# Perceiver-style block on one core: heads stage without its tile loop, two-half probabilities times values, GpSimd and VectorE splitting the rotary sums by Q and K, late code loads on ScalarE's queue

## What is computed

```python
x = x + xattn(layernorm(x), ctx, wq, wk, wv, wo)      # one head, 256 context rows and the 64 own rows
# 16 heads of 128, rotary, causal, 64 tokens a sequence
Q, K, V = xn @ W_Q[n] + b_Q, xn @ W_K[n] + b_K, xn @ W_V[n] + b_V
r1, r2 = x1 * cos - x2 * sin, x1 * sin + x2 * cos     # for Q and for K
probs = softmax(where(causal, Q @ K.T / sqrt(128), -inf))
x = x + (probs @ V) @ W_O + b_O
# gate, up and down weights are 4-bit codes with a scale for each group of 128
y = (silu(xn @ w_gate.T) * (xn @ w_up.T)) @ w_down.T
x = x + y / sqrt(mean(y * y) + eps)
```

## Time and profile before

| | us |
|---|---|
| median of 3 runs (1444.58 to 1448.53) | 1446.46 |
| profiled execution | 1445.04 |
| its span in the trace | 1443.2 |
| TensorE busy in the span | 1360.7 (94%) |
| VectorE busy | 980.1 (68%) |
| ScalarE busy | 508.1 (35%) |
| GpSimd busy | 425.7 (29%) |

### The profile page before, as it was taken

One profiled execution on the slowest core, in us unless ns is written; L12 is line 12 of the kernel. 1 busy time (PEld: TensorE's weight loads), 2 busy tenths in 40 slices (PEclk: granted clock), 3 DMA queues, 4 the chain that ended last, 5 costly groups with the idle time before them and its releaser, 6 DMA issues. The chain is left out here.

```text
span 1443.2 us, 24076 instructions
## 1 busy us (share of the span) xinstructions
PE 1360.7 (94%) x8964; PEld 795.3 (55%) x8964; DVE 980.1 (68%) x2176; ACT 508.1 (35%) x1249; POOL 425.7 (29%) x302
## 2 busy tenths in 40 slices
PE   8999999968999899998999999999998499999997
PEld 6666666435666566665667666654443234343433
DVE  6443443447887688776877777738829796969693
ACT  3222222322333333332343333320001483838281
POOL 0000000003333133331333333320302391929292
PEclk9999999989999999999999999999999699999999
DMA  8555555331001100101010000268550000000000
GB/s 323 218 212 211 212 196 193 118 126 54 31 28 47 61 30 31 59 16 60 31 59 30 18 28 31 89 199 244 166 157 1 0 2 29 0 29 0 29 1 30
DMA packets 59459, 122.53 MB, mean 85 GB/s; under 512 B 4312, under 2 KB 37720, under 8 KB 52696
## 3 DMA queue, kind: packets, MB, share of 16 engines
q1 hardware_dynamic: 59352, 121.07, 24.5%
HBM read 95.89 MB, written 25.17 MB: 84 GB/s over the span
## 5 line engine op out<-in xcount | busy, mean ns | idle before, releaser
L931 POOL TENSOR_TENSOR hd_rotated<-hd_products 64x512 f32<-64x512 f32 x64 | 109.3, 1708 | 725.1 <-DVE hd_products L1116 725.1
L184 PE MATMUL psum<-hd_xt_hi,hqk_hi 128*128 128x512 f16 x512 | 195.8, 382 | 1.7 <-DVE hd_xt_lo L1090 1.7
L185 PE MATMUL psum<-hd_xt_lo,hqk_hi 128*128 128x512 f16 x512 | 195.6, 382 | 0.0
L186 PE MATMUL psum<-hd_xt_hi,hqk_lo 128*128 128x512 f16 x512 | 195.2, 381 | 0.0
L1442 POOL TENSOR_TENSOR ff_part<-ff_part 128x512 f32<-128x512 f32 x88 | 127.7, 1465 | 98.0 <-DVE ff_part L1569 97.6
L184 PE MATMUL psum<-hd_wv_hi,hd_xt_hi 128*128 128x256 f16 x512 | 140.3, 274 | 4.6 <-DVE hd_wv_lo L1095 4.6
L1471 PE MATMUL psum<-ff_xt_hi,gu 128*128 128x512 f16 x352 | 133.9, 380 | 8.2 <-DVE w_rows L1607 3.3
L185 PE MATMUL psum<-hd_wv_lo,hd_xt_hi 128*128 128x256 f16 x512 | 140.3, 274 | 0.0
L186 PE MATMUL psum<-hd_wv_hi,hd_xt_lo 128*128 128x256 f16 x512 | 140.2, 274 | 0.0
L1472 PE MATMUL psum<-ff_xt_lo,gu 128*128 128x512 f16 x352 | 133.4, 379 | 0.0
L1569 DVE SCALAR_TENSOR_TENSOR ff_part<-psum,gu_scale,ff_part 128x512 f32<-128x512 f32 x176 | 119.8, 738 | 6.2 <-ACT ff_part L1519 3.6
(11 more groups left out here) (170 smaller groups left out, 2795.0 us busy)
## 6 DMA issues: line engine op xcount, KB each, us to landing
xa_kv_t<-in_ctx_t_dram SPq DMA_DIRECT2D x16, 1024.0 KB, 5.3
xa_kv<-in_ctx_dram SPq DMA_DIRECT2D x16, 1024.0 KB, 4.8
w_rows<-in_head_weights_dram SPq DMA_DIRECT2D x12, 1024.0 KB, 7.5
z_scratch<-hd_z_hi SPq DMA_DIRECT2D x32, 256.0 KB, 2.2
z_scratch<-hd_z_lo SPq DMA_DIRECT2D x32, 256.0 KB, 2.5
w_rows<-z_scratch SPq DMA_DIRECT2D x8, 1024.0 KB, 8.0
hqk_lo<-z_scratch SPq DMA_DIRECT2D x8, 1024.0 KB, 7.7
xn<-in_x_dram SPq DMA_DIRECT2D x8, 512.0 KB, 3.8
```

The source lines that it names most:

```text
L184: pe.matmul(out, lh, rh, start=(first and i == 0), stop=False)
L185: pe.matmul(out, lh, rl, start=False, stop=False)
L186: last = pe.matmul(out, ll, rh, start=False, stop=(final and i == k - 1))
L931: pool.tensor_tensor(rotated[0:HALF, w, 0, :], products[0:HALF, w, 0, :], products[0:HALF, w, 2, :], ALU.subtract)
```

## The change

The change has four parts.

- **Heads without the loop.** `for_each_step` calls the steps of all four tiles one by one. Tokens and counts are constants, and the `nop`s that followed waits on registers are gone.
- **Probabilities times values in halves.** ScalarE writes the transposed probabilities and the values as float16 (`pt_hi`, `v_hi`) and no longer frees their banks. VectorE makes the rest: `low_values` (two instructions, behind `low_top`) and `low_probs` (two instructions, between k0's and k1's products), and these free banks 5, 6 and 7. z is 24 float16 matmuls of 128 columns in place of 8 products in float32.
- **Sums.** `rotate` becomes `multiply` and `sum_up`: GpSimd makes all four sums of Q, VectorE all four of K, after k1's products. TensorE's scores wait for one count of each.
- **Late codes.** Groups 2 and 3 are loaded by two DMAs at the head of ScalarE's list, each behind `gu_decoded` alone.

The diff, cut to its core:

```diff
-        v = sb("v", [P, TT, 2 * DH], F32)
+        v_hi, v_lo = sb("v_hi", [P, TT, 2 * DH], F16), sb("v_lo", [P, TT, 2 * DH], F16)
 
         probs = sb("probs", [P, SEQS, S], F32)
 
-        probs_t = sb("probs_t", [P, 2, TT, P], F32)
...
                 for pair in range(PAIRS):
                     ends = pair == PAIRS - 1
                     step(Step(t, pair, turn_next=ends and not last_tile, proj=not (ends and last_tile), last_tile=last_tile))
-            with eng.Fori(0, NT - 1) as t:
-                tile(t, False)
-            tile(NT - 1, True)
+            for t in range(NT):
+                tile(t, t == NT - 1)
+
+        def sum_up(eng, w):
+
+            low, high = slice(0, HALF), slice(HALF, P)
+            eng.tensor_tensor(rotated[low, w, 0, :], products[low, w, 0, :], products[low, w, 2, :], ALU.subtract)
+            eng.tensor_tensor(rotated[high, w, 0, :], products[low, w, 1, :], products[low, w, 3, :], ALU.add)
+            eng.tensor_tensor(rotated[low, w, 1, :], products[high, w, 0, :], products[high, w, 2, :], ALU.subtract)
+            return eng.tensor_tensor(rotated[high, w, 1, :], products[high, w, 1, :], products[high, w, 3, :], ALU.add)
 
         block = ctx.enter_context(nc.Block())
 
...
         def _(pool):
             def step(s):
                 if not s.proj:
                     return
-                for w in range(2):
-                    banks.wait_moved(pool, s.runs_proj, ("qk"[w], 1))
-                    if not isinstance(s.t, int):
-                        pool.nop(nofuse=True)
-                    pool.tensor_tensor(rotated[0:HALF, w, 0, :], products[0:HALF, w, 0, :], products[0:HALF, w, 2, :], ALU.subtract)
-                    pool.tensor_tensor(rotated[HALF:P, w, 1, :], products[HALF:P, w, 1, :], products[HALF:P, w, 3, :],
-                                       ALU.add).then_inc(pool_rotated, 1)
-
-            for_each_step(nc.gpsimd, step)
+                banks.wait_moved(pool, s.runs_proj, ("q", 1))
+                sum_up(pool, 0).then_inc(pool_rotated, 1)
+
+            for_each_step(step)
 
         @block.tensor
         def _(pe):
...
-                    pe.wait_ge(rotated_done, s.a * 2 + 2)
-                    pe.wait_ge(pool_rotated, s.a * 2 + 2)
+                    pe.wait_ge(rotated_done, s.a + 1)
+                    pe.wait_ge(pool_rotated, s.a + 1)
                     if not s.proj:
...
                         for i in range(TT):
-                            last = pe.matmul(psum_of(unit)[:, i * P:(i + 1) * P], v[:, i, h * DH:(h + 1) * DH], probs_t[:, h, i, :],
-                                             start=True, stop=True)
+                            d = slice(h * DH, (h + 1) * DH)
+                            last = three_passes(pe, psum_of(unit)[:, i * P:(i + 1) * P], [(v_hi[:, i, d], v_lo[:, i, d])],
+                                                [(pt_hi[:, h, i, :], pt_lo[:, h, i, :])])
                         banks.fills(last, unit)
...
                     for n in range(2):
                         keys = slice(n * S, (n + 1) * S)
                         turned = psum_of(s.probs)[keys, :].rearrange("p (i h q) -> p h i q", h=2, q=S)
-                        last = act.activation(probs_t[keys, :, :, keys], turned, ACT.Copy)
-                    banks.moves(last, s.probs)
+                        last = act.activation(pt_hi[keys, :, :, keys], turned, ACT.Copy)
+                    last.then_inc(pt_hi_done, 1)
                     for h in range(2):
                         banks.wait_filled(act, s.runs_z, (s.z, h))
                         if h == 0:
                             act.wait_ge(small_loaded_z_stored, s.a * 32 + 16 * HEADS_SMALL)
-                            act.nop(nofuse=True)
                         act.activation(z_hi[:, h, :], psum_of((s.z, h)), ACT.Identity,
                                        bias=bias_v[:, s.pair * 2 + h:s.pair * 2 + h + 1]).then_inc(z_hi_done, 1)
                 if s.proj:
                     for half in range(2):
                         unit = ("v", half)
                         banks.wait_filled(act, s.runs_proj, unit)
-                        banks.moves(act.activation(v[:, 2 * half:2 * half + 2, :].rearrange("p i d -> p (i d)"), psum_of(unit), ACT.Copy,
-                                                   scale=AS / (XS * WS)), unit)
+                        act.activation(v_hi[:, 2 * half:2 * half + 2, :].rearrange("p i d -> p (i d)"), psum_of(unit), ACT.Copy,
+                                       scale=AS / (XS * WS)).then_inc(v_hi_done, 1)
                 if s.pair == WO_STEP - 1:
                     act.wait_ge(loaded[0], s.t * 16 + 32)
-                    act.activation(wo_hi[:, bass.ds(s.t * 4, 4), :].rearrange("p n m -> p (n m)"), w_rows[:, 0, :], ACT.Copy,
+                    act.activation(wo_hi[:, s.t * 4:s.t * 4 + 4, :].rearrange("p n m -> p (n m)"), w_rows[:, 0, :], ACT.Copy,
                                    scale=WS).then_inc(wo_hi_done, 1)
 
             act.wait_ge(bias_scaled, 2)
             act.wait_ge(zeros_set, 1)
 
-            for_each_step(nc.scalar, step)
+            for_each_step(step)
 
         @block.vector
         def _(dve):
...
-            def rotate(s, w):
+            def multiply(s, w):
                 for half, (first, second) in enumerate((((cos, 0), (sin, 1)), ((sin, 2), (cos, 3)))):
                     unit = ("qk"[w], half)
+                    if s.att and w == 1 and half == 1:
+                        low_probs(s)
                     banks.wait_filled(dve, s.runs_proj, unit)
                     for tab, slot in (first, second):
                         last = dve.scalar_tensor_tensor(by_sequence(products[:, w, slot, :]), by_sequence(psum_of(unit)),
                                                         bias[:, w, half, s.next_pair:s.next_pair + 1], table(tab), ALU.add, ALU.mult)
                     banks.moves(last, unit)
-                banks.wait_moved(dve, s.runs_proj, ("qk"[w], 1))
-
-                low, high = slice(0, HALF), slice(HALF, P)
-                dve.tensor_tensor(rotated[high, w, 0, :], products[low, w, 1, :], products[low, w, 3, :], ALU.add)
-                dve.tensor_tensor(rotated[low, w, 1, :], products[high, w, 0, :], products[high, w, 2, :],
-                                  ALU.subtract).then_inc(rotated_done, 1)
+
+            def low_values(s):
+                for half in range(2):
+                    unit = ("v", half)
+                    runs = {"turn": s.turns, "proj": s.a}
+                    dve.wait_ge(v_hi_done, 2 * s.a + half + 1)
+                    at = slice(2 * half, 2 * half + 2)
+                    banks.moves(dve.scalar_tensor_tensor(v_lo[:, at, :].rearrange("p i d -> p (i d)"), psum_of(unit), AS / (XS * WS),
+                                                         v_hi[:, at, :].rearrange("p i d -> p (i d)"), ALU.mult, ALU.subtract), unit)
+
+            def low_probs(s):
+                dve.wait_ge(pt_hi_done, s.a + 1)
+                for n in range(2):
+                    keys = slice(n * S, (n + 1) * S)
+                    turned = psum_of(s.probs)[keys, :].rearrange("p (i h q) -> p h i q", h=2, q=S)
+                    last = dve.tensor_tensor(pt_lo[keys, :, :, keys], turned, pt_hi[keys, :, :, keys], ALU.subtract)
+                banks.moves(last, s.probs)
 
             def while_exponentials_run(s):
                 if s.pair in (1, 2, 3) and not s.last_tile:
...
                     banks.moves(last, s.scores)
                     banks.wait_moved(dve, s.runs_scores, s.scores)
                     dve.tensor_scalar(low_top[:, :], top[:, :], -HEAD_SCALE, None, ALU.mult).then_inc(low_top_ready, 1)
+                    low_values(s)
                     while_exponentials_run(s)
                     dve.wait_ge(exp_done, s.a + 1)
                     dve.reciprocal(inv_total[:, :], total[:, :]).then_inc(inv_done, 1)
...
-                    rotate(s, 0)
-                    rotate(s, 1)
+                    multiply(s, 0)
+                    multiply(s, 1)
+                    banks.wait_moved(dve, s.runs_proj, ("k", 1))
+                    sum_up(dve, 1).then_inc(rotated_done, 1)
+                else:
+                    low_probs(s)
                 if s.att:
...
-            def load_codes(g):
-                sp.dma_start(codes[g % 2], codes_of(gu_codes, g)).then_inc(gu_loaded[g % 2], 16)
-
             def load_x1(t):
                 sp.dma_start(x2[:, t * TT:(t + 1) * TT, :],
                              x1_rows[t * TILE:(t + 1) * TILE, :].rearrange("(b p) d -> p b d", p=P)).then_inc(x1_loaded, 16)
 
             load_z(1, 0)
...
-                    if half == 0:
-                        sp.wait_ge(gu_decoded, t - 1)
-                        load_codes(t)
 
         @block.gpsimd
         def _(pool):
...
+            for g in range(2, KD):
+                act.wait_ge(gu_decoded, g - 1)
```

(3 more changed lines are left out.)

28 lines of the change are left out of this document (12 added, 16 removed).

## The result

The changed kernel takes **1434.77 us** (median of 4 runs, 1433.5 to 1435.27) against 1445.83 for the kernel before beside it (1444.58 to 1448.53): ratio 0.9919, 95% interval 0.9905 to 0.9933. It is faster, by 11 us; I had forecast 34, and the result lies 0.8 us above my range. The profiled execution took 1435.27 us; its span is 1433.5 against 1443.2, so 9.7 less. I cut both spans at three starts on TensorE.

The account below looks back on a forecast made before the run. TensorE, busy for 94% of the span, and its waits bound the kernel. Terms -13.0 - 13.7 + 18.6 + 0 - 2.0 - 23.1 - 1.0 = -34.2 took 1445.0 to 1410.8, median 1412 us; range 1393 to 1434.

Parts of the forecast that it names:

- The loop: Heads: straight code removes the surplus at the loop's two jumps, -13.0 us, bounds 0 and -13.0.
- Rival 3: Heads: straight code pauses too, since its instructions are still fetched; +13, 1425 us, chance 0.07.
- z in three passes: Heads: z's 24 matmuls of 128 columns take 1.35 us instead of 1.78, over 32 steps -13.7 us.
- rival 2: Heads: weight loads set z's pace; up to +33, 1445 us, halfway 1428; chance 0.15.
- Low halves: Heads: z waits for VectorE's `low_probs`, 0.22 us in plain steps, more in late ones; +18.6 us, bounds 0 and +37.
- Rivals 1: Heads: the low halves cost nothing, as VectorE is idle for several us of a step; 1393 us, chance 0.12.
- 5: Heads: GpSimd's sums of Q block `low_probs`; +56, 1468 us, slower than before; chance 0.05.
- Sums: Heads: sums of Q and K finish before the scores are due; 0, with 0.7 us of cover.
- First scores: Start of heads: TensorE waited 5.72 us for GpSimd's K sums; the new split ends sooner, -2.0 us.
- Feed-forward: Feed-forward's first dozen transposes run at 2.4 GHz instead of starting at the 1.2 GHz level; -1.0 us.
- Late codes: Merge: earlier code loads end VectorE's pauses and most of TensorE's 24.20 us wait; -23.1 us, bounds 0 and -24.2.
- rival 4: Merge: codes early in vain, z's loads late or VectorE not done before TensorE; 1435 us, chance 0.06.

Follow-up runs that it names:

- Run 5: The kernel before with its tile loop written out and nothing else changed: 1432.49 us, ratio 0.9889.
- run 11: The changed kernel with half of the next pair's values ahead of z, late codes behind z's landing, and z back in float32: 1410.11 us, ratio 0.9744.
- run 6: The changed kernel with TensorE doing half of the next pair's values (24 matmuls) ahead of z: 1413.85 us, ratio 0.9745.
- run 7: The changed kernel with each late code load issued only once the z needed next has landed: 1414.87 us, ratio 0.9772.
- run 10: The kernel before with only the late codes moved to ScalarE's queue, each behind the landing of z: 1425.49 us, ratio 0.9845.
- run 9: The changed kernel with half the values ahead of z, codes behind z, and fifteen down loads issued after tile 2's first z half: 1401.89 us, ratio 0.9667.
- run 3: The changed kernel with each late code load cut by columns into eight, packets of 1,408 bytes instead of 11,264: 1425.43 us, ratio 0.9856.

## Why the prediction was right in its parts and wrong in its sum

- **The loop, -13.0: right.** Run 5 shows it alone: heads of 621.6 instead of 634.3, and its first step was 0.4 longer than before. Rival 3 falls.
- **z in three passes, -13.7: right,** 0.45 us a step, 14.3 in 32; run 11 has 14.7. The pace is 0.0556, on the line through 512 and 256 columns. The weight loads stay hidden, and rival 2 falls. The 81 ns of the Trainium skill (TensorE: Matmul & The Clock Gate, section Back-to-back issue gap) for 128 columns with a load for each matmul is not what this stream shows; the measurement decides.
- **Low halves, +18.6: right in sum,** 19.3 by run 6, where nothing but this wait was covered, and in part by luck, since errors offset each other. Pairs 1 and 2 were late by 1.2 and 0.9 (I had 1.5 and 1.1), pair 4 by 0.5 (I had 1.2), and a plain step by 0.49 where I had 0.22, which is +4 us over 15 steps against -4 in the pairs. In a plain step ScalarE's copy ends at 598.19, the subtractions run from 598.23 to 599.62, and z starts at 599.88: 0.30 for the two hand-overs where I had 0.1, and 1.39 for the subtractions where I had 1.31. Rivals 1 and 5 fall.
- **Sums, 0: right;** no scores waited for them behind the first. **First scores, -2.0: not resolved.** The -1.3 lies in the spread of this start among the runs (332.3 to 336.0), and the first step is 21.90 instead of 20.91, so that 0.3 is left at the second scores.
- **Feed-forward, -1.0: right,** -1.2.
- **Late codes, -23.1: wrong,** +0.1. The step that failed is the sentence "The loads now compete with loads of z, whose landing ahead of their use I can only bound by the idle they cause now, none". No idle means only that z lands in time; it says nothing of how much later it may land. I took it as cover, and gave the collision 0.06 as a part of rival 4, whose time, 1435, is the one that came.

  The cover could have been read from the kernel before: z(1,1) landed at 1001.41 and was used at 1009.84, so 8.4 us. From the first issue to the last landing it took 12.1 us there and 42.0 after the change, 29.9 more. Less the 8.4 of cover that is 21.5, and the idle is 21.33.

  The merge's sum by the runs: -23.15 for the idle ahead of the feed-forward, +21.33 for z(1,1), thirteen matmuls at half clock, 13 x (0.426 - 0.216) = +2.7, and -0.85 for the wait on VectorE at 1088.55 that is gone; that is +0.1, as measured. That VectorE would be ready was right: its idle of 26.56 ahead of group 3 is gone, and 1.05 is left ahead of the feed-forward. The 7 us of slack are not shown. Once z comes in time (runs 7 and 10) the term is -20.7 and -18.4.

The remaining sum of the prediction would have been met: run 7, the change as forecast with the collision taken away, stands at 1414.87 where I had 1412.

What stays open: the spread of the start of the heads (332.3 to 336.0 among the runs), which no edit explains, run 9's one fast execution, and what z waited for while half of the DMA engines' time was free.

## What to carry to other kernels

Before a load is moved to a second queue so that it starts earlier, write down for each load then in flight how long it takes and how far ahead of its use it lands: that distance is the cover, and not the absence of idle. Here it was 8.4 us, and the load became 29.9 us longer. If two streams must meet, hold the one that has time until the urgent one has landed, and cut its packets to the other's size. And where a new wait of TensorE for a short vector operation appears in each step, look for TensorE work of a later step that can stand in front of it: 2.6 us of values moved gave 19 us back.

## What the runs showed of the hardware that I had not expected

From 984 to 996 a load of codes kept a pace of 35 to 41 packets of 11,264 bytes in 4 us, whatever stood beside it. From 988 to 992 it went 41 to 41 with the packets of the other queue and so took nine tenths of the bytes. The Trainium skill (DMA: Bandwidth & Descriptors, section Queues, rings and completion order) says that each DMA engine goes round the queues and drains a whole packet of one before it turns to the next. The 41 to 41 fits that rule; the 361 to 35 and 155 to 39 beside it, and the 746 to 288 of run 3, neither show nor refute it, since the view doesn't tell the engines apart. The whole rate fell as well: 133 GB/s in that stretch, which is what a load of codes almost alone moved in the kernel before; 292 with packets of 1,408 bytes (run 3), 341 with no late codes in flight (run 7, 982 to 990, loads of z, x and down codes):

```profile
DMA packets 2376, 2.73 MB, mean 341 GB/s; under 512 B 38, under 2 KB 2051, under 8 KB 2376
```

And the issuing engine is held while such loads are in flight: the same two issues of z(1,1) took 13.56 us with the codes in flight and 0.98 without, so that all that stood behind them on SyncE was late too. Why it is held, no run shows.
